# Two-block x products in another order, filler products on TensorE, expert weights loaded from another queue, first scores ahead of the last tokens

## The chip, the cores and the metric

The kernel runs on one core of a Trainium2 chip, written out instruction by instruction for the five engines: TensorE (PE, matmuls), VectorE (DVE), ScalarE (ACT), GpSimd (POOL) and SyncE (SP, transfers). The metric is the device time of one execution in microseconds.

## What is computed

x has the shape (8, 64, 128, 64): batch, channel, time, variable. The reference is a token embedding, an attention and a mixture of experts, each of the last two with a residual and a layer norm:

```python
# tokens: patches of 16 steps with stride 8, their real DFT, times W
x_emb = concat([xf.real, xf.imag]) @ W.T          # (B, V*N, 64)
# attention over all 8192 tokens, on normalised rows
f = l2norm(h); attn = softmax(f @ f.T)
att = l2norm(f * 0.8 + (attn @ f) * 0.2)
h = layernorm(h + att)
# feed-forward: 8 experts of 64x64, top 2, exact gelu
out = tokens + sum_e combine[:, e] * (gelu(tokens @ w1[e] + b1[e]) @ w2[e] + b2[e])
h = layernorm(h + out)
```

## The kernel before

The DFT is folded into W first: PE transposes the raw W in 72 small records, and DVE then makes four slices of effective weights, `weff[:, s]`, one for each of the four time steps s of a half patch. It counts them in `s_weff`.

x comes in eight blocks, one for each batch element, of two halves of 1 MB; SP issues the half on partitions 0 to 63 and ACT the other, into a ring of three (`xring`). From block 3 on, an issue waits until the block three before it is used up (`s_prod`, raised at the last product of a block). For each block PE makes eight products (two column halves q, four slices s), which are accumulated in two banks of PSUM. Each product is an fp32 matmul over 512 columns and stands in the trace as two records. The first two blocks are woven together by `first_products`: slice by slice, block 0 and then block 1. ACT copies each finished block to `prod` (`s_prodev`). `tokens(i)` transposes the sums back, in banks 4 to 7, and DVE adds the two parts to h (`s_h`). After the first two blocks PE does one product for the edge column (`xedge`) and one for a bias (`b2raw`).

From h come the norms (a square on ACT, a sum on DVE, a power on POOL), the normalised rows f, and their high and low fp16 parts in `fs` (`high_of_f` on ACT, the low part on POOL). SP transposes `fs` eight tokens' worth at a time by DMA into `hilo` (`transposed(i)`) and copies it with its halves exchanged into `lohi` (`swapped(i)`, two transfers). Tile i of the two is wanted from step c = 4i of the attention on.

The attention runs over 512 slots of scores of 128 tokens by 1,024. A step c of PE's loop holds two slots: twelve matmuls for each (`scores`), and the sums of the exponentials of earlier slots (`high_sums`, `low_sums`). ACT makes the Exp of each slot, DVE its low part (L879). The banks of slot 0 are those of the even blocks' products, the banks of slot 1 those of the odd ones'. The tables `LATE_SQUARES`, `LATE_HIGHS` and `LATE_NORMS` say ahead of which slot ACT and DVE do the norm work of the last tiles that is left (slot: tile). The feed-forward part follows behind the attention; it reads `w1s`, `routers`, `w2s` and `b1s`, which are loaded at the start of the program by POOL's queue, each twice, for partitions 0 to 63 and 64 to 127.

Every engine works its instructions off in the written order, and semaphores set the rest.

## Time and profile before

| | us |
|---|---|
| median of 3 runs | 908.37 |
| lowest, highest | 902.75, 910.06 |
| the profiled execution | 904.54 |
| its span in the trace | 902.7 |
| PE busy | 870.8 (96%) |
| DVE busy | 767.4 (85%) |
| ACT busy | 650.3 (72%) |
| POOL busy | 171.4 (19%) |

The busy shares are averages over the three stages: products and tokens to about 85 us, attention to about 787, feed-forward to the end. The page's row PEclk gives the clock that TensorE was granted, in tenths of full speed. All times in the trace are counted from the start of the span.

### The profile page before, as it was taken

How to read it: one execution, taken by the hardware profiler on the slowest of the kernel's cores; microseconds unless marked ns; L12 is line 12 of the kernel's file. 1: busy time of each engine (PE TensorE's matmuls, PEld its weight loads, DVE VectorE, ACT ScalarE, POOL GpSimd, SP SyncE). 2: the span in 40 equal slices, each digit the busy share in tenths (PEclk: the TensorE clock that was granted, in tenths of full speed). 3: DMA queues.
4: the chain of work that ended last, by engine and by line, in shares of the span. 5: the costliest groups of instructions: out<-in, count | busy, mean ns of one | idle time of the engine just before them, and what ended most of it. 6: DMA issues, size and time to landing. Idle time of an engine off the chain costs nothing.

```text
span 902.7 us, 30612 instructions
## 1 busy us (share of the span) xinstructions
PE 870.8 (96%) x13276; PEld 438.0 (49%) x13276; DVE 767.4 (85%) x921; ACT 650.3 (72%) x1260; POOL 171.4 (19%) x184
## 2 busy tenths in 40 slices
PE   3998999999999999999999999999999999899995
PEld 2444455555555555555555555555555555444331
DVE  5244999999899899989998998899899899778983
ACT  0124887888778788878887878778778788567763
POOL 3045500000220000000000000000000899736213
PEclk9899999999999999999999999999999999989998
DMA  9798410000000000000000000000000000000011
GB/s 276 186 286 145 72 37 3 3 2 3 3 3 3 2 3 2 3 3 3 2 3 3 3 3 3 2 3 3 3 2 2 3 2 3 2 0 21 17 24 36
DMA packets 28710, 26.53 MB, mean 29 GB/s; under 512 B 9536, under 2 KB 26176, under 8 KB 28576
## 3 DMA queue, kind: packets, MB, share of 16 engines
q1 hardware_dynamic: 19408, 14.98, 7.4%
q10 hardware_dynamic: 8752, 8.93, 3.8%
q8 instruction: 105, 1.72, 0.8%
q0 software_dynamic: 416, 0.66, 0.4%
q14 instruction: 29, 0.24, 0.1%
HBM read 18.28 MB, written 2.10 MB: 23 GB/s over the span
## 4 chain that ended last, share of the span: by engine, by line
PE 92%; DVE 3%; DMA 2%; ACT 1%; issue 1%; POOL 0%; SPq 0%; POOLq 0%; DVEq 0%; ACTq 0%
PE ps L443 36%; PE ps L460 25%; PE ps L473 12%; PE ps L376 6%; PE ps L529 4%; PE ps L596 3%; DMA ring<-in_x_dram 2%; PE ps L486 2%; DVE ring L879 1%; PE ps L585 1%; PE ps L612 1%; PE ps L507 1%; ACT ring L779 1%; PE ps L498 1%; PE ps L411 1%
## 5 line engine op out<-in xcount | busy, mean ns | idle before, releaser
L879 DVE TENSOR_TENSOR ring<-ring 128x1024 f16<-128x1024 f32 x512 | 602.6, 1227 | 47.2 <-ACT ring L779 46.9
L779 ACT ACTIVATE ring<-ps 128x1024 f32<-128x1024 f32 x512 | 519.3, 1020 | 132.9 <-PE ps L443 132.6
L443 PE MATMUL ps<-big 64*64 64x512 f16 x6144 | 375.2, 376 | 2.2 <-ACT ring L779 2.0
L460 PE MATMUL ps<-ring,fs 64*64 64x512 bf16 x4096 | 274.4, 384 | 0.0
L443 PEld LDWEIGHTS ps<-big 64*64 64x64 f16 x6144 | 171.6, 106 | 164.4 <-ACT ring L779 5.1
L460 PEld LDWEIGHTS ps<-ring,fs 64*64 64x64 f16 x4096 | 116.1, 106 | 109.9
L473 PE MATMUL ps<-ring,fs 64*64 64x512 f16 x2048 | 153.5, 376 | 0.1
L779 ACT ACTIVATION_READ_ACCUMULATOR ring<-ps 128x1 f32 x512 | 101.3, 198 | 0.0
L325 POOL TENSOR_SCALAR stat<-stat 128x16 f32<-128x16 f32 (+2 forms) x4 | 1.9, 466 | 449.7 <-DVE stat L928 449.4
L473 PEld LDWEIGHTS ps<-ring,fs 64*64 64x64 f16 x2048 | 58.4, 107 | 53.2 <-PE ps L460 1.1
L376 PE MATMUL ps<-ring,weff 128*128 128x512 f32 x128 | 61.1, 636 | 8.8 <-DMA ring<-in_x_dram 8.6
L744 ACT ACTIVATE ring<-ps,b1s 128x512 f32<-128x512 f32 x64 | 40.4, 683 | 25.5 <-PE ps L529 25.5
L1010 DVE TENSOR_TENSOR ring<-ring,ps 128x512 f32<-128x512 f32 x64 | 41.0, 682 | 15.0 <-ACT ring L744 11.2
L376 PEld LDWEIGHTS ps<-ring,weff 128*128 128x128 f32 x128 | 25.4, 203 | 40.9 <-issue 30.3
L666 ACT ACTIVATE sums<-ps 128x1024 f32<-128x1024 f32 x8 | 8.2, 1024 | 46.5 <-PE ps L376 46.5
L529 PE MATMUL ps<-big,w1s 64*128 64x512 f32 x128 | 37.1, 657 | 0.1
L596 PE MATMUL ps<-ring,w2s 128*64 128x512 f32 x128 | 35.1, 627 | 0.8 <-DVE ring L1010 0.8
L316 POOL TENSOR_TENSOR stat<-stat 128x16 f32<-128x16 f32 (+2 forms) x4 | 5.2, 1291 | 146.5 <-DVE stat L923 146.5
L859 DVE TENSOR_REDUCE h<-ps 128x512 f32<-128x1024 f32 x8 | 9.7, 1219 | 25.3 <-PE ps L411 25.3
L357 POOL TENSOR_TENSOR stat<-stat,cst 128x8 f32<-128x8 f32 x8 | 13.1, 1635 | 53.7 <-DVE stat L942 53.7
L486 PEld LDWEIGHTS ps<-cst,sums 128*128 128x128 f32 x128 | 16.1, 197 | 10.3 <-issue 7.4
L486 PE MATMUL ps<-cst,sums 128*128 128x65 f32 x128 | 18.4, 288 | 2.6 <-DVE sums L884 2.6
(135 smaller groups left out, 461.6 us busy)
## 6 DMA issues: line engine op xcount, KB each, us to landing
ring<-in_x_dram ACTq DMA_DIRECT2D x8, 1024.0 KB, 14.8
ring<-in_x_dram SPq DMA_DIRECT2D x8, 1024.0 KB, 13.3
big<-big SPq DMA_DIRECT2D x16, 128.0 KB, 2.4
out_dram<-h SPq DMA_DIRECT2D x16, 128.0 KB, 2.4
f<-in_L_tok_W_dram SPq DMA_DIRECT2D x1, 288.0 KB, 4.1
fs<-consts_dram ACTq DMA_DIRECT2D x1, 256.0 KB, 22.4
xedge<-in_x_dram POOLq DMA_DIRECT2D x2, 128.0 KB, 7.2
w1s<-in_L_ffn_w_dram POOLq DMA_DIRECT2D x2, 128.0 KB, 7.5
```

What stands on the lines that cost most here:

```text
L357: gt(stat[:, INV_OUT, sl(z)], stat[:, VAR_OUT, sl(z)], minus_half, ALU.pow).then_inc(s_istd2, 1)
L376: return mm(bank(2 * (b % 2) + q).rearrange("p (m v) -> p m v", v=V), weff[:, s, :], xring[:, b % XR, 8 * q:8 * q + 8, s, :], start=(s == ...
L443: last = mm(bank(SLOT_BANK[slot_of(s)] + r)[m:m + 64, :], of_k[r][:, 128 * k + m:128 * k + m + 64], of_q[r][:, q0 + 512 * r:q0 + 512 * r + ...
L460: last = mm(bank(sums_bank(s // NT) + half)[m:m + 64, :], fs[64 * r:64 * r + 64, s % NT, m:m + 64], probs[64 * r:64 * r + 64, s % 8, :].bi ...
L473: last = mm(bank(sums_bank(s // NT) + half)[64 * e:64 * e + 64, :], fs[64 * r:64 * r + 64, s % NT, 0:64], probs_lo[64 * r:64 * r + 64, s % ...
L486: last = mm(part_bank(x, b)[:, (D + 1) * k:(D + 1) * (k + 1)], outT[:, 128 * t:128 * t + 128], centred_both, start=True, stop=True)
L529: last = mm(bank(r), w1s[rows, 128 * i:128 * i + 128], hT[rows, BLK * y:BLK * y + BLK], start=True, stop=True)
L596: last = mm(bank(4)[64 * n:64 * n + 64, :], w2s[:, i, :], hidc[:, (2 * u + n) % 4, :], start=(i == 0), stop=False, skip_group_check=True)
L744: a(hid[:, (2 * u + r) % 4, :], bank(r), ACT.Gelu, bias=b1s[:, u % 4:u % 4 + 1]).then_inc(s_gelu, 1)
L779: a(probs[:, s % 8, :], bank(SLOT_BANK[slot_of(s)], 2), ACT.Exp, accum_out=rowsum[:, s:s + 1]).then_inc(s_pr, 1)
L879: tt(probs_lo[:, s % 8, :], probs[:, s % 8, :], probs[:, s % 8, :].bitcast(BF16)[:, 1:2 * QC:2], ALU.subtract).then_inc(s_lo, 1)
L1010: tt(hidc[:, i, :], hid[:, i, :], bank(2 + r), ALU.mult).then_inc(s_hw, 1)
```

## The change

It consists of six edits. `first_products` takes the pairs (block, slice) in a listed order, in which slices 0 to 2 of block 0 come ahead of block 1's. `kept_busy(n)` is new: n products of the identity with itself, 128 columns, into bank 7, where nothing is read before the edge product writes it; 14 of them stand between the fold and the first product, 4 and 6 behind slices 0 and 1 of block 0. The eight loads of expert weights go from POOL's queue to SP's, behind the last block of x. The edge column's loads on POOL wait for block 1 of x, and no longer for the first slice of `weff`. `scores(0)` stands ahead of the tokens of blocks 6 and 7, and waits for `s_prodev` of block 6 alone. The three tables of late norm work move to later slots.

```diff
--- before.py
+++ after.py
@@ -32,9 +32,10 @@
 BATCHES = ((0, 1), (1, 3), (3, 5), (5, 8))
 BATCH_AT = (3, 12, 21)
 EARLY = 2
-LATE_SQUARES = {2: 6, 3: 7}
-LATE_HIGHS = {4: 5, 14: 6, 22: 7}
-LATE_NORMS = {1: 6, 4: 7}
+BUSY_AHEAD, BUSY_BEHIND = 14, (4, 6)
+LATE_SQUARES = {4: 6, 7: 7}
+LATE_HIGHS = {6: 5, 18: 6, 26: 7}
+LATE_NORMS = {6: 6, 9: 7}
 NS = NQ * NT
 NC = NQ * PAIRS
 SLOT_BANK = (0, 2)
@@ -250,6 +251,16 @@
                     sp.wait_ge(s_prod, b - XR + 1)
                 sp.dma_start(xring[0:64, b % XR, :, :, :].rearrange("p m s v -> p m (s v)"),
                              x_h[b, 0]).then_inc(s_xb[b % XR], 16)
+            sp.wait_ge(s_zero, 3)
+            for half in range(2):
+                rows = slice(64 * half, 64 * half + 64)
+                sp.dma_start(w1s[rows].rearrange("p (e k) -> p e k", e=E),
+                             w1.rearrange("e d k -> d e k")).then_inc(s_w, 16)
+                with nc.allow_non_contiguous_dma(reason="512 floats"):
+                    sp.dma_start(routers[rows, E * half:E * half + E], router_w.rearrange("e d -> d e")).then_inc(s_w, 16)
+                sp.dma_start(w2s[rows], w2[half:E:2].rearrange("i k o -> k i o")).then_inc(s_w1r, 16)
+                with nc.allow_non_contiguous_dma(reason="512 floats"):
+                    sp.dma_start(b1s[rows], b1[half:E:2].rearrange("i k -> k i")).then_inc(s_w1r, 16)
             for i in range(NG):
                 transposed(i)
             swapped(NG - 1)
@@ -267,18 +278,11 @@
             pool.memset(routers[:, :], 0.0).then_inc(s_zero, 1)
             pool.memset(comb[:, :, :, :], 0.0).then_inc(s_zero, 1)
             pool.memset(halves_of[:, :], -0.5).then_inc(s_zero, 1)
-            pool.wait_ge(s_zero, 3)
-            pool.wait_ge(s_weff, 1)
+            pool.wait_ge(s_xb[1], 16)
+            pool.wait_ge(s_xc[1], 16)
             for half in range(2):
                 rows = slice(64 * half, 64 * half + 64)
                 pool.dma_start(xedge[rows], x[:, :, T - 1, :].rearrange("b c v -> c b v")).then_inc(s_xe, 16)
-                pool.dma_start(w1s[rows].rearrange("p (e k) -> p e k", e=E),
-                               w1.rearrange("e d k -> d e k")).then_inc(s_w, 16)
-                with nc.allow_non_contiguous_dma(reason="512 floats"):
-                    pool.dma_start(routers[rows, E * half:E * half + E], router_w.rearrange("e d -> d e")).then_inc(s_w, 16)
-                pool.dma_start(w2s[rows], w2[half:E:2].rearrange("i k o -> k i o")).then_inc(s_w1r, 16)
-                with nc.allow_non_contiguous_dma(reason="512 floats"):
-                    pool.dma_start(b1s[rows], b1[half:E:2].rearrange("i k -> k i")).then_inc(s_w1r, 16)
             pool.dma_start(b2raw[:, :], b2).then_inc(s_b2r, 16)
             pool.wait_ge(s_cst, 16)
             nc.gpsimd.tensor_copy(ident16[:, :], ident).then_inc(s_id16, 1)
@@ -380,16 +384,21 @@
                 pe.wait_ge(s_xb[b % XR], 16 * (b // XR + 1))
                 pe.wait_ge(s_xc[b % XR], 16 * (b // XR + 1))
 
+            def kept_busy(n):
+                for i in range(n):
+                    mm(bank(7)[:, 0:128], ident, ident, start=True, stop=True)
+
             def first_products():
-                for s in range(HALF):
+                for b, s in ((0, 0), (0, 1), (0, 2), (1, 0), (1, 1), (1, 2), (0, 3), (1, 3)):
                     pe.wait_ge(s_weff, s + 1)
-                    for b in range(2):
-                        if s == 0:
-                            loaded(b)
-                        for q in range(2):
-                            last = product(b, q, s)
-                        if s == HALF - 1:
-                            last.then_inc(s_prod, 1)
+                    if s == 0:
+                        loaded(b)
+                    for q in range(2):
+                        last = product(b, q, s)
+                    if s == HALF - 1:
+                        last.then_inc(s_prod, 1)
+                    if b == 0 and s < 2:
+                        kept_busy(BUSY_BEHIND[s])
 
             def products(b):
                 loaded(b)
@@ -413,6 +422,7 @@
                                   ident[64 * s:64 * s + 64, 64 * s:64 * s + 64], is_transpose=True, start=True, stop=True)
                 last.then_inc(s_tr, 1)
 
+            kept_busy(BUSY_AHEAD)
             first_products()
             pe.wait_ge(s_xe, 32)
             pe.wait_ge(s_wpad, 1)
@@ -426,10 +436,6 @@
                 if b % 2 == 0:
                     tokens(b - 2)
                     tokens(b - 1)
-            tokens(B - 2)
-            tokens(B - 1)
-            pe.wait_ge(s_prodev, B)
-
             highs = (hilo[0:64, :], lohi[64:128, :])
             lows = (lohi[0:64, :], hilo[64:128, :])
 
@@ -550,6 +556,13 @@
                         pe.wait_ge(s_pr, NQ * NT - 1)
                         up(0)
 
+            pe.wait_ge(s_hilo[0], 16)
+            pe.wait_ge(s_lohi[0], 32)
+            pe.wait_ge(s_prodev, B - 1)
+            scores(0)
+            tokens(B - 2)
+            tokens(B - 1)
+            pe.wait_ge(s_prodev, B)
             for c in range(NC + 3):
                 t = c % PAIRS
                 crossed = c % 2 == 1
@@ -558,12 +571,13 @@
                     beside((c - 1) // PAIRS, (c - 1) % PAIRS)
                 if c == 1:
                     pe.wait_ge(s_h, NG)
-                if c < PAIRS and t % 4 == 0:
+                if 0 < c < PAIRS and t % 4 == 0:
                     i = t // 4
                     pe.wait_ge(s_hilo[i % 2], 16 * (i // 2 + 1))
                     pe.wait_ge(s_lohi[i % 2], 32 * (i // 2 + 1))
+                if 0 < c < NC:
+                    scores(2 * c)
                 if c < NC:
-                    scores(2 * c)
                     scores(2 * c + 1)
                 if crossed and c >= 3:
                     pe.wait_ge(s_straight, c // 2)
```

How this moves instructions is seen at three places. The first is PE's order from the fold to the second block of the loop. In the rows L369 (L373 after) are the fold, L376 (L380) the products of x, L389 the filler, L419 and L423 (L429, L433) the edge and the bias. With their waits, before:

```order
L369 MATMUL ps<-cst,f 64x64 x35
L376 MATMUL ps<-ring,weff 128x512 [waits s_xc0,s_x0,s_weff]
L376 MATMUL ps<-ring,weff 128x512
L376 MATMUL ps<-ring,weff 128x512 [waits s_xc1,s_x1]
L376 MATMUL ps<-ring,weff 128x512
L376 MATMUL ps<-ring,weff 128x512 [waits s_weff]
L376 MATMUL ps<-ring,weff 128x512 x3
L376 MATMUL ps<-ring,weff 128x512 [waits s_weff]
L376 MATMUL ps<-ring,weff 128x512 x3
L376 MATMUL ps<-ring,weff 128x512 [waits s_weff]
L376 MATMUL ps<-ring,weff 128x512 x3
L419 MATMUL ps<-xedge,wpad 128x512 [waits s_wpad,s_xe]
```

and after:

```order
L373 MATMUL ps<-cst,f 64x64 x35
L389 MATMUL ps<-cst 128x128 x14
L380 MATMUL ps<-ring,weff 128x512 [waits s_xc0,s_x0,s_weff]
L380 MATMUL ps<-ring,weff 128x512
L389 MATMUL ps<-cst 128x128 x4
L380 MATMUL ps<-ring,weff 128x512 [waits s_weff]
L380 MATMUL ps<-ring,weff 128x512
L389 MATMUL ps<-cst 128x128 x6
L380 MATMUL ps<-ring,weff 128x512 [waits s_weff]
L380 MATMUL ps<-ring,weff 128x512
L380 MATMUL ps<-ring,weff 128x512 [waits s_xc1,s_x1,s_weff]
L380 MATMUL ps<-ring,weff 128x512
```

Block 1's wait (s_xc1, s_x1) stood behind one slice of block 0 and stands behind three, and filler stands in three places.

The second place is SP's queue behind the loads of x. Before:

```order
L251 DMA ring<-in_x_dram 64x16x256 x8
L245 DMA_TRANSPOSE big<-fs 128x8x128
L237 DMA big<-big 64x1024 x2
L245 DMA_TRANSPOSE big<-fs 128x8x128
L237 DMA big<-big 64x1024 x2
```

and after:

```order
L252 DMA ring<-in_x_dram 64x16x256 x8
L257 DMA w1s<-in_L_ffn_w_dram 64x8x64
L260 DMA routers<-in_L_ffn_router_w_dram 64x8x1
L261 DMA w2s<-in_L_ffn_w_dram 64x4x64
L263 DMA b1s<-in_L_ffn_b_dram 64x4x1
L257 DMA w1s<-in_L_ffn_w_dram 64x8x64
L260 DMA routers<-in_L_ffn_router_w_dram 64x8x1
L261 DMA w2s<-in_L_ffn_w_dram 64x4x64
L263 DMA b1s<-in_L_ffn_b_dram 64x4x1
L246 DMA_TRANSPOSE big<-fs 128x8x128
L238 DMA big<-big 64x1024 x2
```

Eight transfers have come between block 7 and the first transpose of f.

The third is PE's passage from the last products (L376, after L380) over the tokens (L411, after L420) to the scores (L443, after L449). Before:

```order
L376 MATMUL ps<-ring,weff 128x512 x16
L411 MATMUL ps<-cst,sums 128x64 x32
L376 MATMUL ps<-ring,weff 128x512 x8
L411 MATMUL ps<-cst,sums 128x64 x32
L443 MATMUL ps<-big 64x512 x72
L460 MATMUL ps<-ring,fs 64x512 x16
```

and after:

```order
L380 MATMUL ps<-ring,weff 128x512 x16
L420 MATMUL ps<-cst,sums 128x64 x32
L380 MATMUL ps<-ring,weff 128x512 x8
L449 MATMUL ps<-big 64x512 x12
L420 MATMUL ps<-cst,sums 128x64 x32
L449 MATMUL ps<-big 64x512 x60
L466 MATMUL ps<-ring,fs 64x512 x16
```

Twelve of the 72 score matmuls, those of slot 0, have come ahead of the last 32 token transposes.

## Rows read from the trace of the kernel before

**Rows 1.** The page, part 4: shares of the chain that ended last.
```profile
PE 92%; DVE 3%; DMA 2%; ACT 1%; issue 1%; POOL 0%; SPq 0%; POOLq 0%; DVEq 0%; ACTq 0%
```

**Rows 2.** Timeline of PE, 0 to 80: start, duration, what.
```profile
5.00 4.10 PE L369 MATMUL ps<-cst,f 64*64 64x64 f32 x72 [5.00 <-DMA f<-in_L_tok_W_dram]
...
21.47 15.16 PE L376 MATMUL ps<-ring,weff 128*128 128x512 f32 x28 [4.26 <-DMA ring<-in_x_dram]
36.47 1.02 PE L419 MATMUL ps<-xedge,wpad 128*128 128x512 f32 x2
...
46.20 13.97 PE L376 MATMUL ps<-ring,weff 128*128 128x512 f32 x32
...
76.31 4.13 PE L376 MATMUL ps<-ring,weff 128*128 128x512 f32 x9
```

**Rows 3.** Windows view: stretch, length, busy times (instructions), clock, DMA share, GB/s.
```profile
13.40:17.30 3.90, 3.72 (x4) 1.17 (x4) 3.73 (x8) 1.49 (x2) 3.90 (x6) 1.00 1.09 346
17.30:27.30 10.00, 5.83 (x7) 2.52 (x8) 6.80 (x15) 0.00 (x0) 3.80 (x7) 0.66 1.14 245
21.40:27.30 5.90, 5.83 (x7) 2.52 (x8) 2.91 (x7) 0.00 (x0) 0.00 (x0) 0.50 1.14 236
27.30:36.40 9.10, 9.10 (x22) 3.99 (x21) 0.00 (x0) 0.84 (x1) 0.61 (x1) 1.00 0.22 53
```

**Rows 4.** The chain in order of time, 0 to 30: start, duration.
```profile
1.99 19.44 DMA ring<-in_x_dram
```

**Rows 5.** Timeline of DVE, 11 to 24.
```profile
19.70 0.22 DVE L836 TENSOR_TENSOR weff<-h 128x64 f32<-128x64 f32 x1
...
23.20 0.22 DVE L836 TENSOR_TENSOR weff<-h 128x64 f32<-128x64 f32 x1
```

**Rows 6.** DMA issues in 34.9 to 35.5, microseconds to landing.
```profile
ring<-in_x_dram ACTq DMA_DIRECT2D x1, 1024.0 KB, 11.2
```

**Rows 7.** DMA issues in 16.8 to 17.5, microseconds to landing.
```profile
xedge<-in_x_dram POOLq DMA_DIRECT2D x1, 128.0 KB, 7.7
```

**Rows 8.** The page, parts 3 and 6: queues' packets, issues.
```profile
q0 software_dynamic: 416, 0.66, 0.4%
...
big<-big SPq DMA_DIRECT2D x16, 128.0 KB, 2.4
```

**Rows 9.** Timeline of all engines, 28 to 62.
```profile
30.66 0.61 POOL L286 CAST sel<-fs 128x512 f16<-128x512 f32 x1 [9.55 <-DMA cst<-consts_dram]
...
34.95 0.56 ACTq L642 DMA_DIRECT2D ring<-in_x_dram  x1
...
60.21 0.56 ACTq L642 DMA_DIRECT2D ring<-in_x_dram  x1
60.78 8.12 SPq L245 DMA_TRANSPOSE big<-fs  x1
```

**Rows 10.** DMA issues in 60.5 to 70, microseconds to landing.
```profile
ring<-in_x_dram ACTq DMA_DIRECT2D x1, 1024.0 KB, 15.0
```

**Rows 11.** Timeline of all engines, 75 to 100.
```profile
75.81 1.16 SPq L237 DMA_DIRECT2D big<-big  x2
...
83.48 1.02 ACT L666 ACTIVATE sums<-ps 128x1024 f32<-128x1024 f32 x1 [2.10 <-PE ps L376]
84.41 0.62 ACT L660 ACTIVATE fs<-f 128x512 f16<-128x512 f32 x1
...
85.31 2.35 DVE L859 TENSOR_REDUCE h<-ps 128x512 f32<-128x1024 f32 x2 [2.86 <-PE ps L411]
...
85.70 1.49 PE L443 MATMUL ps<-big 64*64 64x512 f16 x24
...
86.59 1.02 ACT L779 ACTIVATE ring<-ps 128x1024 f32<-128x1024 f32 x1 [1.57 <-PE ps L443]
...
97.22 1.02 ACT L779 ACTIVATE ring<-ps 128x1024 f32<-128x1024 f32 x1 [0.84 <-PE ps L443]
...
99.85 1.02 ACT L779 ACTIVATE ring<-ps 128x1024 f32<-128x1024 f32 x1 [0.51 <-PE ps L443]
```

## The prediction

> **What bounds the kernel now.** I read the page first: in the chain that ended last TensorE (PE) holds 92% [rows 1]. So I looked for the stretches in which PE waits or runs slowly, and then in the timeline for what ends each. There are two at the start, and the change works on both.
>
> The first is the products of x blocks 0 and 1. PE finishes the 72 fold records at 9.10 us (5.00 + 4.10), does block 0's first slice from 13.4 on, and waits until 21.47 for block 1, whose SP half lands at 1.99 + 19.44 = 21.43 [rows 2, 4]. Only then do 28 records follow, and they end when the next line starts, at 36.47: 15.0 us. A record at full speed costs 0.43 us (32 of them, for blocks 3 and 4, took 13.97 with the last drain); 28 would be 12.0 us. The other 3.0 us are the clock: in 21.4 to 27.3 it was granted at 0.50, half of 2.4 GHz, and 7 records took 5.83 us; from 27.3 on it is 1.00 and 22 took 9.1 [rows 3]. The four records in 13.4 to 17.3 also took 3.72 us, 0.9 each, which is the half clock, though the view writes 1.00 there. Both slow starts follow over 4 us of idle PE.
>
> The second is the step from products to attention. PE has done block 7 when ScalarE (ACT) starts its copy at 83.48; the first scores start at 85.70, the first Exp at 86.59, and the regular beat of 2.63 us for two slots is reached with the Exp of slot 8 at 97.22 [rows 11]. The beat is that between the Exps of slots 8 and 10, and it is PE's own work.
>
> **Part by part.**
>
> *The order of the first 16 products.* Before, slices 1 to 3 of block 0 wait behind block 1's load. In the new order block 0's slices 0, 1 and 2 go first. Slice 2's weights are there at 19.70 + 0.22 = 19.92 [rows 5]; its two products are four records, 1.7 us, so PE is through at 21.65, just when block 1 lands. What is left is five pairs, (1,0), (1,1), (1,2), (0,3), (1,3): 20 records, 20 x 0.43 = 8.6 us at full clock. End at 30.25 and not 36.47: **6.2 us less**. Of that 3.4 us are the eight records taken out from behind the load and 3.0 the clock, less 0.2 for the start. The last slice's weights come at 23.42 [rows 5], before slice 3 is wanted at 26.8, so VectorE (DVE) holds nothing.
>
> *The filler.* Fourteen 128-column fp32 products are 28 records. The trace has none of this form; by columns one is a quarter of 0.43, so 0.107 us, and double at half clock: 3.0 to 6.0 us, from 9.10 to 12.1 or 15.1. The first slice's inputs are complete at 13.4. At the high end it starts 1.7 us late, and with the two later fillers (8 and 12 records, 0.9 and 1.3 us) slice 2 ends near 22.4, 0.7 us past block 1's landing. At the low end nothing is late: the filler of 4 ends at 16.0, a little before the next weights (3.5 us ahead of the 19.92, at 16.4), the filler of 6 at 19.4. I take 0, since PE has worked since 5.00 and in the later case rose to full speed 5.8 us after its start at 21.47 [rows 3]. Whether the clock stays full is the open point. The Trainium skill ("TensorE: Matmul & The Clock Gate", the section on the HAM clock gate) says that the throttled state is the default and that activity releases it. The trace agrees with half clock after both idle stretches, but no row shows whether short products like these count; if they do not, the sum loses the clock's share, 3.0 us.
>
> *What is late next there.* Block 0 is released about 1.7 us ahead of block 1, as before, so all later loads move earlier by the same 6.2 us. Block 3 is the tight one: its ACT half is issued at 34.95 and lands 11.2 us later, at 46.15, and PE takes it at 46.20 [rows 2, 6, 9]. Both ends move together, so no gain is lost. Block 2 is wanted from 31.5. In 27.3 to 36.4 the engines moved 53 GB/s, 0.48 MB [rows 3], which is 1.4 us at their 346, so it was there soon after 28.7; it comes no later with the weights gone from its way. The edge column xedge is now issued by GpSimd (POOL) when block 1 is there, 21.4, with 0.6 us for an issue (ACT's row, [rows 9]) or up to 1, and 7.7 us to landing [rows 7]: the second lands at 29.7 to 30.1, against a need at 30.25. b2raw behind it comes at 30.3 to 31.1, against 31.2. The late constants, for which POOL waits until 30.66 now [rows 9], are wanted at 31.2. All three just fit; they can cost up to 1 us if the load stretches.
>
> *The weights on SP.* Eight transfers leave POOL's queue at 14 to 20 us and go to SP's, behind block 7 and ahead of all eight transposes of f. Over both halves w1 has 1,024 runs of 256 bytes and w2 512, the router 1,024 single numbers of 4 bytes and b1 512: 0.39 MB in 3,072 pieces, 96 long and 96 short ones for each of 16 engines. Their cost w stands in front of the first transpose. Low bound: bytes alone, 0.39 MB at 346 GB/s, 1.1 us. Nearest row: when POOL's queue carried them (with xedge, 0.66 MB), 17.3 to 27.3 moved 245 GB/s and not 346 [rows 3], so 1.0 MB was lost, 2.9 us. But that queue bundled its pieces into 416 packets [rows 8]. High bound: each piece costs what a 1 KB piece of x costs an engine, 16 x 1,024 bytes at 346 GB/s = 47 ns, so 192 x 47 = 9.1 us. I take w = 5, between the last two.
>
> What waits for it: the first transpose is issued at 60.78, its instruction holds SP for 8.12 us because the queue is full with block 7, and its data are there at 75.81 when the swap of tile 0 is issued; the second of its two copies goes 0.6 us later and lands in 2.4, at 78.8 [rows 8, 9, 11]. The first scores start at 85.70. They are moved to 83.45, so the slack is 4.6 us. **w = 5 costs 0.4 us** against it; at 9.1 it is 4.5 us. Tile 1 is wanted only four steps, 10.5 us, after tile 0. Block 7's ACT half lands at 60.21 + 15.0 = 75.2, PE takes the block at 76.31 [rows 2, 9, 10]: 1.1 us of slack against the pieces that now share the engines with it.
>
> The Trainium skill ("DMA: Bandwidth & Descriptors", Issuing engines are not separate DMA queues) says that all queues run on the same 16 engines, and that issuing elsewhere saves only issue time. By that rule the move of the weights is worth nothing by itself, only its new time and place count; I give it no gain either, since block 1's landing is no longer what the sum hangs on.
>
> *The first scores moved up.* scores(0) needs no copy of block 7. It runs from 83.45, under the copy; the Exp of slot 0 then follows ACT's high part (84.41 + 0.62) at 85.05 and not at 86.59. But slot 2 still waits for the last token reduction, which DVE ends at 85.31 + 2.35 = 87.66 [rows 11], so most of the 1.5 us is swallowed. Going on slot by slot with ACT's 1.1 us and 0.9 us from scores to Exp: slot 4's Exp comes at 91.2 (one square of 0.5 us ahead of it instead of two squares and a high part), slot 6 at 93.9, slot 8 at 96.6 against 97.22 now. **0.6 us less.** Bounds: 0 if ACT's moved squares and DVE's moved norms bite at slots 6 to 9, 2.2 us if slot 8 came as much earlier as the first scores. The later high parts (slots 18 and 26 for 14 and 22) serve tiles first wanted at slots 48 and 56, and ACT has 0.5 us of idle in each beat: nothing.
>
> **The sum.** -6.2 - 0.6 + 0.4 = -6.4 us. The profiled execution took 904.54 (span 902.7), so it would take 898.1. The three timed runs have their median 3.8 us above that execution, at 908.37, and reach from 902.75 to 910.06. From the median the sum gives 902.0; I say **900**, between the two.
>
> **Rivals.**
>
> 1. *The forecast*: about 6.4 us, 898 to 902. Chance 0.50.
>
> 2. *The queue takes the wait's place.* w is near 9, the first transpose comes 4.5 us late, and scores(0), which now stands ahead of the tokens of blocks 6 and 7, holds these too. Gain 6.8 - 4.5 = 2.3, time 904. For it: every piece a packet, the full queue at 60.78. Against: 2.9 us for the same data in POOL's queue. Chance 0.17.
>
> 3. *The filler does not hold the clock.* Then seven of the 20 records go at half clock, and the end is 33.2: gain 3.4, time 903. For it: 72 short fold records from 5.00 on did not keep PE fast at 13.4. Against: it had 4.4 us of idle between. Chance 0.11.
>
> 4. *More comes free*: w costs nothing, and slot 8 comes as much earlier as the first scores do, 85.70 - 83.45 = 2.2 us: 6.2 + 2.2 = 8.4, time 898, and under 897 with half the scatter of the runs. Against: the token reduction's end. Chance 0.14.
>
> 5. *Slower than before.* The same queue, with 4-byte pieces that cost far more than a 1 KB piece. It decides from w = 4.6 + 6.8 = 11.4 us on; over 1% slower needs w above 20.5, about 190 ns for each of the 96 four-byte pieces of an engine. With w = 22 PE waits 17.4 us for tile 0 and the kernel takes 900 + 0.4 - 0.8 + 17.4 = 917. The rows show nothing of 4-byte pieces in SP's queue. Chance 0.08, and 0.05 for over 1%.
>
> **Range and chances.** 1 to 4 hold 0.92; the scatter of the runs shown, 4 us to either side, lies over each. 893.5 to 907 leaves out the slower case and the ends of the scatter. A measurement of this kernel can tell about 1%, 9.1 us, from no change; the forecast lies below that. Faster by over 1%: some scatter of cases 4 and 1, 0.17. Slower by over 1%: 0.05. Within: 0.78.
>
> **What would show it.** In the changed profile PE's first block-1 product should start within 1 us of the landing of block 1's second half, PE's clock should read 1.00 from there to the end of the first products, and these should end near 30.3. xedge must have landed there. The first transposes should be issued after eight weight transfers, and their data be there 6 us before now, less what is over the slack: scores(0) should start near 77 and end its wait with PE's own work, not with a DMA. If its releaser is a DMA of big, case 2 or 5 holds, and the time from block 7's last product to scores(0) is their price. The beat should stay 2.63 us. The forecast is wrong if the products end after 31, or scores(0) starts after 79.

## The result and the profile after

The changed kernel took 903.32 us (median of 17 runs, 897.63 to 905.49), the kernel before 908.38 in the runs beside it (902.07 to 910.82). The ratio is 0.9954, with a 95% interval from 0.9933 to 0.9974: faster by 0.46%, clear of noise, and half of the 0.9% that the forecast of 900 meant against the median before. The profiled execution took 900.97 with a span of 898.9, so 3.6 and 3.8 us less than before.

The page's chain after, as [rows 1]:

```profile
PE 94%; DVE 3%; ACT 1%; issue 1%; DMA 0%; POOL 0%; POOLq 0%; DVEq 0%; ACTq 0%
```

PE has 2% more of it and the DMA engines have none: the wait for block 1 is gone. PE's timeline over the first products, as [rows 2] (start, duration, what):

```profile
9.03 5.38 PE L389 MATMUL ps<-cst 128*128 128x128 f32 x28
14.25 1.93 PE L380 MATMUL ps<-ring,weff 128*128 128x512 f32 x4
...
19.96 10.47 PE L380 MATMUL ps<-ring,weff 128*128 128x512 f32 x24
30.26 1.02 PE L429 MATMUL ps<-xedge,wpad 128*128 128x512 f32 x2
```

and the windows, as [rows 3] (stretch, length, busy times, clock, DMA share, GB/s):

```profile
17.30:21.40 4.10, 4.10 (x20) 2.63 (x19) 3.89 (x9) 0.00 (x0) 0.94 (x1) 1.00 1.09 347
21.40:27.30 5.90, 5.90 (x16) 2.55 (x15) 2.73 (x7) 0.00 (x0) 1.58 (x4) 1.00 0.98 192
```

The rows left out between them are filler and the second slice, without a gap. PE does not wait for block 1, the clock is at 1.00 behind block 1 where [rows 3] have it at half, four records take 1.9 us with their drain and not 3.7, and the edge product starts at 30.26 where it was 36.47. The forecast had 30.25. The filler ran until 14.41 and block 0 was complete at 14.13, so it held the first slice up by 0.1 us. Slice 2 starts at 19.96, when its weights are there (19.73), and is done at 21.7; block 1 had landed at 20.16, before PE wanted it.

SP's queue, as [rows 9, 11]:

```profile
68.83 1.33 SPq L246 DMA_TRANSPOSE big<-fs  x1
72.06 1.16 SPq L238 DMA_DIRECT2D big<-big  x2
```

The weights stand in front of the first transpose, and the swap that waits for it starts at 72.06. Against the products' end that is 41.8 us and was 39.3, so w was 2.5 us, near the 2.9 of the nearest row, and within the slack of 4.6.

The passage to the attention, as [rows 11]:

```profile
77.14 0.84 PE L449 MATMUL ps<-big 64*64 64x512 f16 x12
...
78.68 1.02 ACT L793 ACTIVATE ring<-ps 128x1024 f32<-128x1024 f32 x1
...
89.95 1.03 ACT L793 ACTIVATE ring<-ps 128x1024 f32<-128x1024 f32 x1
```

scores(0) starts at 77.14 and waits for nothing; slot 0's Exp comes at 78.68, 7.9 us earlier than before, and slot 8's at 89.95, 7.3 us earlier. At that point the change had won more than the 6.8 that the forecast had for it (6.2 + 0.6); at slot 10 (93.00, before 99.85) it is 6.85. Then it gives back. The Exp of slot 24 comes at 111.48 (118.26 before), that of slot 32 at 123.44 (128.78 before): the lead falls from 6.8 to 5.3 us, and stays at 5.32 until the last Exp at 774.24 (779.56 before). What stands between is on ACT and POOL:

```profile
103.66 7.29 POOL L306 TENSOR_TENSOR fs<-f,fs 128x512 f16<-128x512 f32 x1 [8.51 <-ACT fs L674]
110.92 2.61 POOL L302 TENSOR_TENSOR stat<-stat,cst 128x8 f32<-128x8 f32 x1
113.61 1.61 POOL L304 TENSOR_TENSOR f<-h,stat 128x512 f32<-128x512 f32 x1
```

```profile
115.25 0.63 ACT L674 ACTIVATE fs<-f 128x512 f16<-128x512 f32 x1 [1.65 <-POOL f L304]
```

ACT stands idle for 1.65 us until POOL has f of tile 7, since the high part of tile 7 is written ahead of slot 26. POOL is late because the low part of tile 6 held it for 7.29 us, an operation whose median is 1.16 us over its eight executions. Before, the same low part took 1.48 us, and f of tile 7 was there 4.1 us ahead of its high part:

```profile
109.33 1.60 POOL L300 TENSOR_TENSOR f<-h,stat 128x512 f32<-128x512 f32 x1
```

```profile
115.00 0.63 ACT L660 ACTIVATE fs<-f 128x512 f16<-128x512 f32 x1
```

The last stage gives back the rest: 123.16 us from the last Exp to the end before, 124.67 after. There the clock falls:

```profile
784.60:794.90 10.30, 10.30 (x31) 3.78 (x30) 5.62 (x18) 5.64 (x16) 0.00 (x0) 0.50 0.00 0
```

Before it was at 0.50 for a shorter time:

```profile
788.50:795.30 6.80, 6.80 (x26) 3.89 (x24) 2.30 (x8) 3.02 (x8) 0.00 (x0) 0.50 0.00 0
```

### The profile page after: what moved, and what is told of

Same layout as the page of the kernel before. It is cut to its first block, busy times and chain, and to the rows that moved or that the text cites. A ratio compares the mean times of both kernels' runs of the same rounds, so it can differ in the third digit from the quotient of the medians.

```text
span 898.9 us, 30708 instructions
## 1 busy us (share of the span) xinstructions
PE 875.5 (97%) x13324; PEld 445.4 (50%) x13324; DVE 768.5 (85%) x921; ACT 650.5 (72%) x1260; POOL 169.7 (19%) x176
## 4 chain that ended last, share of the span: by engine, by line
PE 94%; DVE 3%; ACT 1%; issue 1%; DMA 0%; POOL 0%; POOLq 0%; DVEq 0%; ACTq 0%
PE ps L449 36%; PE ps L466 25%; PE ps L479 12%; PE ps L380 6%; PE ps L535 4%; PE ps L610 3%; PE ps L492 2%; DVE ring L893 1%; PE ps L599 1%; PE ps L626 1%; PE ps L513 1%; PE ps L389 1%; ACT ring L793 1%; PE ps L504 0%; PE ps L420 0%
## 5 line engine op out<-in xcount | busy, mean ns | idle before, releaser
L893 DVE TENSOR_TENSOR ring<-ring 128x1024 f16<-128x1024 f32 x512 | 603.3, 1228 | 48.2 <-ACT ring L793 47.9
L449 PE MATMUL ps<-big 64*64 64x512 f16 x6144 | 375.8, 376 | 3.3 <-ACT ring L793 2.0
L449 PEld LDWEIGHTS ps<-big 64*64 64x64 f16 x6144 | 172.3, 106 | 165.7 <-ACT ring L793 6.7
L380 PE MATMUL ps<-ring,weff 128*128 128x512 f32 x128 | 56.5, 596 | 0.1
L380 PEld LDWEIGHTS ps<-ring,weff 128*128 128x128 f32 x128 | 23.8, 190 | 27.7 <-issue 27.5
L680 ACT ACTIVATE sums<-ps 128x1024 f32<-128x1024 f32 x8 | 8.2, 1023 | 39.1 <-PE ps L380 39.1
L306 POOL TENSOR_TENSOR fs<-f,fs 128x512 f16<-128x512 f32 x8 | 15.8, 1971 | 31.4 <-ACT fs L674 31.4
## 6 DMA issues: line engine op xcount, KB each, us to landing
ring<-in_x_dram SPq DMA_DIRECT2D x8, 1024.0 KB, 13.6
```

What stands on the lines that cost most here:

```text
L306: gt(fs[:, sl(i), D:2 * D], f[:, sl(i), :], fs[:, sl(i), 0:D], ALU.subtract).then_inc(s_fs, 1)
L380: return mm(bank(2 * (b % 2) + q).rearrange("p (m v) -> p m v", v=V), weff[:, s, :], xring[:, b % XR, 8 * q:8 * q + 8, s, :], start=(s == ...
L449: last = mm(bank(SLOT_BANK[slot_of(s)] + r)[m:m + 64, :], of_k[r][:, 128 * k + m:128 * k + m + 64], of_q[r][:, q0 + 512 * r:q0 + 512 * r + ...
L893: tt(probs_lo[:, s % 8, :], probs[:, s % 8, :], probs[:, s % 8, :].bitcast(BF16)[:, 1:2 * QC:2], ALU.subtract).then_inc(s_lo, 1)
```

## The experiments

All with 11 to 35 runs of the kernel before on the same chip beside them (its medians there: 907.9 for a1 to a4, 907.1 for b1 to b4, 908.2 for c1 to c4). The checkpoints are read from each kernel's one timeline: the start of the edge product (the first products are done), the Exps of slots 8 and 40 counted from it, the last Exp, and the time from there to the end of the span.

| kernel | edge | slot 8 | slot 40 | last Exp | last stage | clock in the 30 us behind the last Exp | median (range) |
|---|---|---|---|---|---|---|---|
| before | 36.47 | 60.8 | 102.8 | 779.56 | 123.2 | 0.89 | 908.4 (902.1 to 910.8) |
| changed | 30.26 | 59.7 | 103.7 | 774.24 | 124.7 | 0.83 | 903.3 (897.6 to 905.5) |
| a1 changed again | 30.26 | 59.7 | 103.8 | 774.12 | 121.6 | 0.94 | 900.7 (897.7 to 903.3) |
| a2 tile 7 later | 30.06 | 59.6 | 102.2 | 772.39 | 127.5 | 0.72 | 901.4 (896.2 to 902.5) |
| a3 no filler | 30.01 | 60.2 | 104.3 | 774.61 | 126.2 | 0.77 | 902.5 (897.8 to 904.9) |
| a4 old order | 37.67 | 60.1 | 104.1 | 782.07 | 126.2 | 0.77 | 906.7 (903.3 to 910.3) |
| b1 scores alone | 35.26 | 60.3 | 104.5 | 780.13 | 123.2 | 0.89 | 908.4 (905.0 to 910.3) |
| b2 weights alone | 35.97 | 60.6 | 102.7 | 778.92 | 126.3 | 0.77 | 907.4 (901.9 to 909.5) |
| b3 changed, late filler | 30.22 | 59.6 | 103.6 | 774.15 | 120.0 | 1.00 | 896.8 (896.2 to 897.7) |
| b4 late filler and a2 | 30.46 | 59.6 | 102.2 | 772.81 | 120.0 | 1.00 | 895.0 (894.8 to 895.5) |
| c1 before, late filler | 40.63 | 60.7 | 102.8 | 783.84 | 120.0 | 1.00 | 901.6 (899.4 to 905.7) |
| c2 b4, no filler at start | 30.27 | 60.9 | 103.5 | 773.85 | 120.0 | 1.00 | 895.1 (894.5 to 895.8) |
| c3 b3, scores back | 30.62 | 60.8 | 102.9 | 773.91 | 120.0 | 1.00 | 895.7 (895.4 to 896.5) |
| c4 b3, weights on POOL | 30.82 | 61.9 | 106.0 | 777.21 | 120.0 | 1.00 | 898.2 (897.0 to 900.0) |

**a1, the changed kernel again.** No edit.

> The changed kernel once more, unaltered. In its first trace it was 6.8 us ahead of the kernel before at the Exp of slots 10 to 24 and only 5.3 ahead from slot 32 on, because the low part of f's tile 6 held GpSimd for 7.3 us; and 1.5 us more went in the feed-forward part, where the half clock lasted 10.2 us and not 6.8. Theory A: the first loss is built in (tile 7's high part, moved to slot 26, stands 10.5 us behind tile 6's, and GpSimd's three operations between them take longer whenever VectorE leaves it no gap), so ScalarE again waits over 1 us for GpSimd ahead of slot 26. Rival B: 7.3 us was one execution's luck, and the wait is gone here. Both: products of x end near 30.3; time 0.4 to 0.7% under the kernel before; the low-clock stretch in the feed-forward part somewhere between 3 and 11 us.

Ratio 0.9929 (0.9901 to 0.9957). The same operation on POOL:

```profile
103.71 7.29 POOL L306 TENSOR_TENSOR fs<-f,fs 128x512 f16<-128x512 f32 x1 [8.51 <-ACT fs L674]
```

So theory A holds: 7.29 us is no luck. The last stage, 121.6 us here at a mean clock of 0.94, is what differs between the two executions.

**a2, tile 7's high part later.**

```diff
-LATE_HIGHS = {6: 5, 18: 6, 26: 7}
+LATE_HIGHS = {6: 5, 18: 6, 34: 7}
```

> The changed kernel with the high part of f's tile 7 ahead of slot 34 and not 26 (it is wanted at slot 56). Theory A: ScalarE's wait for GpSimd is gone, slots 32 to 500 keep the lead of 6.8 us, and the kernel is 1.5 us (0.15%) faster than the changed one. Rival B (luck) or C (VectorE's own backlog from slot 0 on is what gives the 1.5 us back): the lead falls to 5.3 anyhow and the time equals that of the changed kernel.

Ratio 0.9918 (0.9890 to 0.9946). POOL's operation still took 7.29 us (at 103.41), but ACT does not meet it any more:

```profile
116.51 1.02 ACT L793 ACTIVATE ring<-ps 128x1024 f32<-128x1024 f32 x1 [0.51 <-PE ps L449]
...
123.78 0.63 ACT L674 ACTIVATE fs<-f 128x512 f16<-128x512 f32 x1
```

The 0.51 us of idle ACT are those of the beat, and tile 7's high part has no wait. The last Exp comes at 772.39, 1.85 us earlier, of which 0.2 were there at the products. The median does not show it (901.4 against 900.7), since the last stage scatters by more; b4 against b3 does.

**a3, no filler among the first products.**

```diff
-BUSY_AHEAD, BUSY_BEHIND = 14, (4, 6)
+BUSY_AHEAD, BUSY_BEHIND = 0, (0, 0)
```

> The changed kernel without any filler product (0 ahead, 0 and 0 behind). Theory: the filler holds the clock. Without it PE idles from 9.1 to about 13.4 us, slices 0 to 2 of block 0 run at half clock (3.4 us each, so they end near 24 to 25), and the first products end at 32 to 34, 2 to 4 us later than 30.3; the kernel is 2 to 3.5 us slower than the changed one. Rival: the products of block 0 that now fill the wait hold the clock by themselves; then the end stays within 1 us of 30.3.

Ratio 0.9942 (0.9917 to 0.9967).

```profile
13.96 16.22 PE L380 MATMUL ps<-ring,weff 128*128 128x512 f32 x32 [5.05 <-DMA ring<-in_x_dram]
30.01 1.02 PE L429 MATMUL ps<-xedge,wpad 128*128 128x512 f32 x2
```

```profile
17.30:21.40 4.10, 4.10 (x9) 1.67 (x8) 3.89 (x9) 0.00 (x0) 1.19 (x2) 1.00 1.09 348
```

My theory falls and the rival holds. PE stands still from 8.9 to 13.96 (5.05 us, the first row) and begins at half clock: its records start 0.86 us apart up to the one at 18.36, and 0.43 us apart from 18.86 on, with no filler. (The view writes 1.00 over the slow ones too, as in [rows 3].) With filler, in the changed kernel, they start 0.43 us apart from the first slice on. So the filler does raise the clock, but the time that this saves lies ahead of slice 2, whose weights come at 19.5 to 19.7 in both: slice 2 starts at 19.71 here and at 19.96 with filler. All 32 records are done at 30.01. Block 0's own slices raise the clock before block 1 is wanted.

**a4, the old order with the filler.**

```diff
-                for b, s in ((0, 0), (0, 1), (0, 2), (1, 0), (1, 1), (1, 2), (0, 3), (1, 3)):
+                for b, s in ((0, 0), (1, 0), (0, 1), (1, 1), (0, 2), (1, 2), (0, 3), (1, 3)):
```

> The changed kernel with the first 16 products in the old order (slice by slice, block 0 then block 1), the fillers left in. Theory: 28 records follow block 1's landing at about 20.5 to 21.4 instead of 20; at full clock the products end at 33.5 to 34, at half clock for their first 6 us at 36.5. So 3.4 to 6.2 us of the lead go. Which of the two it is says whether the filler holds the clock over a wait of 5 us for block 1; I expect the half clock, so near 36.

Ratio 0.9995 (0.9966 to 1.0023): the whole gain is gone.

```profile
21.31 6.61 PE L380 MATMUL ps<-ring,weff 128*128 128x512 f32 x8 [3.58 <-DMA ring<-in_x_dram]
27.75 1.50 PE L389 MATMUL ps<-cst 128*128 128x128 f32 x12
...
37.67 1.02 PE L429 MATMUL ps<-xedge,wpad 128*128 128x512 f32 x2
```

```profile
21.40:27.30 5.90, 5.90 (x7) 2.40 (x8) 2.80 (x7) 0.00 (x0) 2.52 (x4) 0.51 1.10 226
```

With the filler but the old order PE idles for 3.6 us before block 1 and runs at half clock until 27.3 all the same, and the filler behind slice 1 costs 1.3 us more. The filler did not keep the clock where it left PE idle for 3.6 us. The order is the change's gain, the filler is not.

**b1, the scores moved alone.**

```diff
-            tokens(B - 2)
-            tokens(B - 1)
-            pe.wait_ge(s_prodev, B)
...
+            pe.wait_ge(s_prodev, B - 1)
+            scores(0)
+            tokens(B - 2)
+            tokens(B - 1)
+            pe.wait_ge(s_prodev, B)
             for c in range(NC + 3):
```

> The kernel before with scores(0) moved ahead of the last tokens, and nothing else (the old tables of late norm work). Theory: the moved scores are worth about 1 us at slot 8 of their own (the changed kernel was 7.3 us ahead there, 6.2 of it from the products). With the old tables ScalarE makes two squares ahead of slots 2 and 3, so I expect slot 0 about 1.7 us earlier than 86.59, slot 8 0.3 to 0.7 us earlier than 97.22, and from slot 32 on a lead of the same size, since the high part of tile 7 stays at slot 22. Rival: the lead at slot 8 is all the tables' work, then it is 0 here. Time within 0.1% of the kernel before either way.

Ratio 1.0020 (0.9997 to 1.0043). Slot 8 comes 0.5 us earlier against the products' end, as expected, but slot 40 comes 1.7 us later:

```profile
104.20 7.29 POOL L302 TENSOR_TENSOR fs<-f,fs 128x512 f16<-128x512 f32 x1 [8.44 <-ACT fs L664]
```

```profile
115.78 0.63 ACT L664 ACTIVATE fs<-f 128x512 f16<-128x512 f32 x1 [1.65 <-POOL f L300]
```

The expectation missed this. The high parts stand where they stood before (slots 14 and 22), and yet the low part of tile 6 takes 7.29 us and ACT waits 1.65. So the moved scores bring it about, also without the new tables. (The new tables with the scores in the old place were not run.) The trace shows one thing more by accident: the half clock behind block 1's landing was shorter here (windows 21.3 to 24.7 at 0.50, 1.00 from there), and the products ended 1.2 us sooner than in [rows 2], though block 1 landed 0.2 us later, at 21.59.

**b2, the weights on SP alone.** The eight transfers as in the change; POOL's wait for the edge column as before.

> The kernel before with the expert weights' eight loads moved to SP's queue behind block 7, and nothing else. Theory: block 1 lands 1 to 2 us earlier (the weights no longer share the engines), so the first products end at 34.5 to 35.5 and not 36.47; tile 0 is ready before the first scores, which wait for nothing. Slot 8 then comes 1 to 2 us before 97.22, and the weights' move has a gain of its own, which the prediction gave it as nought. Rival (the prediction's rule that the engines are shared and only the order counts): the products end within 0.3 us of 36.47. A third way: w is over 6.9 us and slot 0 waits for a DMA of big; the changed kernel's trace speaks against it, with the first transpose's data there at 72.1.

Ratio 1.0000 (0.9972 to 1.0029). Block 1's SP half landed at 1.99 + 19.24 = 21.23, 0.2 us earlier than in [rows 4], and the products end 0.5 us earlier. That is neither the theory's 1 to 2 us nor within the rival's 0.3; the 0.3 that the landing does not explain are a shorter half clock (records 0.85 us apart up to 26.5 and not 27.4). The swap of tile 0 starts at 77.37, 41.4 us behind the products' end and not 39.3: w = 2.1. The rival is the nearer: within 0.3% the move gives and costs nothing here. But 2.1 is the least of w. Read in the same way, the ten traces with the weights in SP's queue have 2.1 to 2.5 (five of them: changed, a1, a2, b2, b3), 3.5 (a3), 3.8 (c2), 3.9 (c3), 4.2 (b4) and 4.8 (a4). What makes the difference is open.

**b3, filler in the feed-forward part's first wait.**

```diff
+BUSY_BETWEEN = 12
...
                     if u < NPAIR * NG:
                         expand(u)
+                    if u == 0:
+                        pe.wait_ge(s_htev, 2)
+                        kept_busy(BUSY_BETWEEN)
```

> The changed kernel with 12 more filler products (24 records, 2.6 us at full clock) between the first expand of the feed-forward part and the product that waits for VectorE's copy of the last sums. Theory: the scatter of all kernels here, 3 us to each side, is the half clock that follows the 2.6 us in which PE waits there; it lasted 3.4 to 17 us in the five traces, and each 3.4 us of it makes the end 1.5 us later. With PE busy in that wait the half clock should be gone or short: from the last Exp to the end 120 to 121.5 us in the trace, where it was 121.6 to 127.5, median 2 to 4 us under the changed kernel's, and a smaller scatter. Rival: the clock falls for the slack of the whole feed-forward part (short products, many small waits) and filler in one gap changes nothing; or the filler itself delays what follows, by up to 1 us.

Ratio 0.9897 (0.9873 to 0.9922).

```profile
780.13 2.94 PE L390 MATMUL ps<-cst 128*128 128x128 f32 x24
782.92 1.00 PE L493 MATMUL ps<-cst,sums 128*128 128x65 f32 x8
```

```profile
784.00:788.00 4.00, 4.00 (x25) 2.18 (x25) 2.52 (x9) 2.98 (x8) 0.00 (x0) 1.00 0.00 0
```

The 24 records fill the wait for DVE's copy, the next product starts at 782.92, 8.77 us behind the last Exp (8.64 in the changed kernel, so the filler delays it by 0.1 us), and the clock stays at 1.00. The last stage takes 120.0 us, and the six runs lie within 1.5 us of each other where the changed kernel's spread over 7.9. In the eight traces without this filler PE waits 2.59 us there, and the length of the last stage goes with its clock in a straight line: 121.6 us at a mean clock of 0.94 over the 30 us, 123.2 at 0.89, 124.7 at 0.83, 126.2 to 126.3 at 0.77 and 127.5 at 0.72. In the changed kernel and its variants this was most of the scatter.

**b4, both.** The edits of a2 and b3.

> The changed kernel with the filler in the feed-forward part's first wait and tile 7's high part ahead of slot 34. Theory: both gains add: 1.6 us at slot 40 and 2 to 4 us behind the last Exp, so a median of 896 to 898 against about 907.9 for the kernel before, ratio 0.987 to 0.990. If the filler does nothing, it is 1.6 us under the changed kernel, ratio 0.991 to 0.994.

Ratio 0.9879 (0.9855 to 0.9902), 1.75 us under b3, as a2's trace said. This version beats the kernel before by 1.2%, and the changed one by 0.6% (a1's median) to 0.9% (903.3).

**c1, the kernel before with the late filler.** The edit of b3, with kept_busy added.

> The kernel before with the 12 filler products in the feed-forward part's first wait, and nothing else. Theory: the long half clock there is what spreads every kernel's runs; so this one should read 120.0 us from the last Exp to the end, as the two kernels with that filler did, 3 us less than the 123.2 of the kernel before's trace, and its runs should lie within 2 us of each other, at 901 to 903. Compared with the changed kernel plus the same filler (896.8) it gives the change's own worth without that noise: 4.5 to 6 us. Rival: the kernel before owes its higher median to something else; then it stays above 904.

Ratio 0.9932 (0.9910 to 0.9954), median 901.6. The last stage is 120.0 us as said, but the runs still spread over 6.3 us and not 2. Its trace, of the slowest of the eight executions (905.69), shows one cause:

```profile
25.69 15.11 PE L377 MATMUL ps<-ring,weff 128*128 128x512 f32 x28 [6.48 <-DMA ring<-in_x_dram]
40.63 1.02 PE L424 MATMUL ps<-xedge,wpad 128*128 128x512 f32 x2
```

```profile
2.00 23.64 DMA ring<-in_x_dram
```

Block 1 landed at 25.64 and not 21.43, and all behind it, the 28 records in 15 us, is as much later. The kernel before hangs on that landing, with nothing to do meanwhile. This is one trace: in the four others with the old order block 1 landed at 21.2 to 21.6, in the nine with the new order at 19.6 to 20.7, and why it comes sooner in these is open. Against b3 the change is worth 901.6 - 896.8 = 4.8 us by the medians, and 3.2 by the two ratios to the kernel before, which was measured anew beside each.

**c2, no filler at the start.** b4 with the edit of a3.

> The changed kernel with the feed-forward filler and tile 7's high part at slot 34, but without the three fillers among the first products. Theory, from the run without fillers (products' end 30.01): they are worth nothing, because block 0's own products fill the wait; the end is within 0.3 us of the 30.2 to 30.5 with them, and the time within 0.5 us of 895.0. Rival: the clock is luck there; then the half clock appears in this trace's first 30 us, and the time is 1 to 3 us over 895.0.

Ratio 0.9867 (0.9835 to 0.9899), median 895.1 against 895.0: the filler among the first products shows no worth in the time. The traces are less even. Slot 8 comes 1.2 us later behind the products' end than in b4 (a3: 0.5 later than in the changed kernel), and block 7's ACT half lands 39.3 us behind that end (a3: 39.1) where b4 and the changed kernel have 37.4 and 37.5. Whether that belongs to the filler is open.

**c3, the scores back.** b3 with scores(0) behind the tokens and the tables of before.

> The changed kernel with the feed-forward filler, the first scores back behind the last tokens and the old tables of late norm work: so the new order of the first products and the weights on SP alone. Theory: the move of the scores gained 1.1 us at slot 8 and lost 1.7 to 1.9 at slots 24 to 32, where GpSimd's low part of tile 6 is kept out by VectorE for 7.3 us. Here it takes 1.5 us again and slot 40 comes 102.7 to 102.9 us after the products' end (103.7 in the changed kernel, 102.8 before), so the time is 0.7 to 1.0 us under 896.8. Rival: the long wait for the port comes here too, since only chance in the timing decides who gets in; then the time is 896.8 or over.

Ratio 0.9874 (0.9842 to 0.9907), 1.1 us under b3. POOL's low part of tile 6 is short again:

```profile
99.38 1.48 POOL L307 TENSOR_TENSOR fs<-f,fs 128x512 f16<-128x512 f32 x1 [6.30 <-ACT fs L673]
```

and slot 40 comes 102.9 us behind the products' end, as before. So in the changed kernel the moved scores with their tables cost 0.7 us by the traces (103.6 in b3) and 1.1 by the medians.

**c4, the weights on POOL, later.** b3 with the eight transfers on POOL behind the edge column and b2raw.

> The changed kernel with the feed-forward filler and the eight weight loads on GpSimd's queue again, but behind the edge column and b2raw, so after block 1 has landed. Theory: the weights' move to SP cost and gained nothing (w was 2.5 us against a slack of 4.6, block 1's landing is not what the products wait for): time within 0.5 us of 896.8, and tile 0's transpose is 2.5 us earlier against the products' end. Rival: on GpSimd's queue they run beside block 3's load, which arrives only just in time; then PE waits 1 to 3 us for it near 40 us and the time is that much over 896.8.

Ratio 0.9902 (0.9867 to 0.9937), median 898.2, 1.4 us over b3, though the two ratios hardly differ (b3 0.9897). What speaks for the rival is the trace, with its last Exp 3.1 us later than in b3:

```profile
39.20 1.21 PE L421 MATMUL ps<-cst,sums 64*128 64x64 f32 x32
42.76 7.53 PE L381 MATMUL ps<-ring,weff 128*128 128x512 f32 x17 [2.35 <-issue]
```

```profile
ring<-in_x_dram SPq DMA_DIRECT2D x1, 1024.0 KB, 10.3
ring<-in_x_dram ACTq DMA_DIRECT2D x1, 1024.0 KB, 13.4
```

PE stands for 2.35 us between the tokens of blocks 0 and 1 and block 3's products, which it did not in the changed kernel. The timeline names no releaser, but the DMA issues do (last column: microseconds to landing): block 3's ACT half, issued at 29.30, lands 13.4 us later, at 42.7; in the changed kernel it took 11.1. The weights, of which the last piece lands at 34.7, run beside it. The theory missed the first transpose too: the swap of tile 0 starts 42.5 us behind the products' end, 0.8 us later than in b3 and not 2.5 earlier, since block 7 itself lands later (its ACT half 41.9 us behind that end, 37.4 in b3).

## Why the prediction was wrong in size

*What bounds the kernel, and the order of the first products (-6.2 us).* Right, in mechanism and size: 36.47 to 30.26, minus 6.21. With the old order put back (a4) all of it goes; without the filler (a3) it stays, and the weights' move alone (b2) brings 0.5. The order was not run by itself. The size has some luck in it: the half clock behind block 1, put at 3.0 us, had varied lengths, and 28 records that take 15.0 us in [rows 2] took 13.6 in b1.

*The filler (0 us, "whether the clock stays full is the open point").* The number was right, the picture was not. I took the filler for what holds the clock and gave case 3 a price of 3 us; in a3 and c2 the clock is full behind block 1 without it, since block 0's own products raise it.

*What is late next.* Right: xedge, b2raw and the constants were there at 30.26 and 31.21. c4 shows how tight block 3's load is.

*The weights on SP (w = 5, 0.4 us).* Mis-sized by half for the changed kernel: w was 2.5 us in it and 2.1 alone, nearer to what POOL's queue showed (2.9) than to a piece's price by x; other variants reach 4.8. It cost nothing, and the rivals 2 and 5 with it fall. The rule of the Trainium skill ("DMA: Bandwidth & Descriptors", Issuing engines are not separate DMA queues) is borne out by b2: queue for queue the move is worth nothing by itself, at a ratio of 1.0000 (0.9972 to 1.0029).

*The first scores moved up (-0.6 us).* The term has the wrong sign. The step that failed is the last sentence of that part, that the high parts serve tiles wanted long after and so cost "nothing": a wait of ACT for POOL was put at nothing, and it took 1.65 us. I compared the slots from which a tile is wanted, and not what the high part itself waits for: ACT does it in order ahead of an Exp, and waits there for f of tile 7, which on POOL stands behind the low part of tile 6. Slot by slot my account was good to slot 8 (96.6 less 6.2 is 90.4, measured 89.95), at slot 10 the change was 0.64 us ahead beyond the products' 6.21, and without ACT's wait the term would have been what I forecast: slot 40 comes 102.2 us behind the products' end in a2 and b4, 102.8 before (c2, which has no wait either but whose slot 8 is 1.2 us late, has 103.5). With the wait it is 103.7, so +0.9 us and not -0.6. It is not the lateness that costs: the high parts of tiles 6 and 7 are eight slots apart in the old tables and in the new, and in b1, with the old ones, the wait is the same and slot 40 comes 104.5 us behind the products' end. b1 and c3 put the cause at the moved scores. Nor could the rows of before have given the wait, had I looked: f of tile 7 was there 4.1 us ahead of its need. It came of the 5.8 us by which POOL's low part grew.

*The sum.* By these terms -6.2 + 0.9 = -5.3 us up to the last Exp; the traces have -5.32. The forecast's own sum was -6.4.

*From the sum to a time.* The second failure. I set 900 "between" two numbers, 2 us under what the sum gave from the median, and called the runs' spread scatter without looking for its place. The runs show two, and both are of the kind that the prediction dealt with elsewhere: the half clock in the last stage (b3), and in the kernel before the landing of block 1 (c1). From the median with the terms as measured, 908.4 - 5.3 = 903.1; measured were 903.3. That this fits to 0.2 us is luck: the changed kernel run again (a1) had 900.7 beside 907.9, 2.6 us lower for the same program, so 900 was missed by less or more from one set of runs to the next. And 903, which rival 3 named, is no point for it, since the clock behind block 1 was full.

*Why POOL takes 7.29 us* is not settled. It took 1.48 to 1.49 in the four kernels with the scores in the old place, whatever the products' order (before, b2, c1, c3), and 7.29 in all ten with the scores moved. In both sorts VectorE goes through its low parts (L893, before L879) nearly without a pause, in the changed kernel 17 in a row:

```profile
95.10 21.20 DVE L893 TENSOR_TENSOR ring<-ring 128x1024 f16<-128x1024 f32 x17
```

One of the 17, looked at by itself:

```profile
109.99 2.05 DVE L893 TENSOR_TENSOR ring<-ring 128x1024 f16<-128x1024 f32 x1
```

The Trainium skill ("SBUF — State Buffer", Who interferes with whom) says that VectorE with two inputs in SBUF and a GpSimd instruction that reads SBUF exclude each other for whole instructions, by order of issue. The trace agrees so far: POOL's operation ends at 110.95, inside that one of the 17, which takes 2.05 us where fifteen others take 1.21 (the last, at 114.23, takes 2.06, and POOL's next operation with two inputs ends in it). That POOL is passed over six times the rule does not say. What the traces add is a coincidence of times. In the ten with 7.29 us POOL's operation begins 0.62 us behind the start of one of VectorE's, and gets through behind a pause of VectorE of 0.05 to 0.09 us, the only one while it lasts; in the four with 1.48 it begins 0.74 to 0.76 us behind, and ends in VectorE's next. So a tenth of a microsecond may decide it. No run here changed that beat alone.

## What to carry to other kernels

When a wait cannot be shortened, look for work of the same engine that does not need what is waited for: here four products (eight records) moved in front of a load were worth 6.2 us, and fillers there nothing that the times show. A filler pays where there is no such work, the clock falls behind the gap, and it fills the gap; find those gaps by the windows view behind each long wait, and in the spread of the runs, which can be a sign of one. For a step that is put off, ask what it waits for at its new place and who stands behind it in the queue, not only when its result is wanted.

## What the runs showed of the hardware

The last stage, the same work in all kernels, lost 1.6 to 7.5 us in eight traces by the length of one stretch of half clock, behind 2.6 us of idle PE (the changed kernel 4.7 in one execution and 1.6 in another); 24 small products in that gap removed it in all six traces that had them. One GpSimd operation of 1.48 us took 7.29 in ten traces of nine kernels to within 10 ns, so a figure that looks like a stray can be part of the program's timing. And the 3,072 small pieces of the weights, half of them of 4 bytes, put back what stood behind them in SP's queue by 2.1 to 4.8 us in ten traces, so by an estimate (192 pieces for each engine) 11 to 25 ns for each piece of an engine.
